# Attention and mixture of experts: group 4's gated rows in the middle stage, final sums partly in halves and partly on TensorE

## What is computed

```python
def _L0_ffn_ref(x, Wg, W1, W2, W3, Ws1, Ws2, Ws3):        # T = 4096 tokens, D = 256, E = 32 experts
    scores = jax.nn.softmax(xf @ Wg, axis=-1)
    weights, indices = jax.lax.top_k(scores, TOP_K)        # TOP_K = 4
    y = jnp.zeros_like(xf)
    for e in range(E):                                     # at most C tokens of each expert
        ...
        out = swiglu(xg, W1[e], W2[e], W3[e]) * w[:, None]
        y = y.at[tok].add(out)
    z = swiglu(xf, Ws1, Ws2, Ws3)                          # the shared expert: silu(x W1) * (x W3) W2
    return (y + z).reshape(B, S, D)

x = x + _L0_xattn_ref(_layernorm(x), ctx, ctx, ...)
x = x + _L0_ffn_ref(_layernorm(x), ...)
```

## Time and profile before

| | |
|---|---|
| median of 3 runs | 789.82 (789.68 to 792.14) |
| the profiled execution | 792.1, its span 790.3 |
| TensorE busy | 747.7 (95%) |
| VectorE busy | 533.0 (67%) |
| ScalarE busy | 465.4 (59%) |
| GpSimd busy | 379.6 (48%) |
| moved by DMA | 164.44 MB, 208 GB/s over the span |
| chain that ended last | TensorE 69%, VectorE 13%, issue 6%, GpSimd 5%, ScalarE 4%, DMA 2% |

### The profile page before, as it was taken

One profiled execution on the slowest core, in us unless ns is written; L12 is line 12 of the kernel. 1 busy time (PEld: TensorE's weight loads), 2 busy tenths in 40 slices (PEclk: granted clock), 3 DMA queues, 4 the chain that ended last, 5 costly groups with the idle time before them and its releaser, 6 DMA issues.

```text
span 790.3 us, 18644 instructions
## 1 busy us (share of the span) xinstructions
PE 747.7 (95%) x4222; PEld 596.3 (75%) x4223; DVE 533.0 (67%) x1683; ACT 465.4 (59%) x1820; POOL 379.6 (48%) x352
## 2 busy tenths in 40 slices
PE   6988999999999999999998959999999999999995
PEld 5766777877777877677775648999999999998555
DVE  4854547575959687686977645666666666665588
ACT  2665777777677868566833204666666666666110
POOL 1002242225747574766567663666666665666000
PEclk9998999999999999999999898999999999999999
DMA  9812072325444454489929788777777675664897
GB/s 311 256 41 63 33 223 96 121 94 170 149 150 140 151 179 136 161 261 355 302 95 367 269 312 265 214 218 246 225 235 240 216 245 182 194 189 142 344 409 323
DMA packets 104734, 164.44 MB, mean 208 GB/s; under 512 B 10902, under 2 KB 87780, under 8 KB 103140
## 3 DMA queue, kind: packets, MB, share of 16 engines
q1 hardware_dynamic: 90447, 120.01, 46.2%
q0 software_dynamic: 13824, 41.96, 14.9%
q10 hardware_dynamic: 404, 1.82, 0.7%
HBM read 90.01 MB, written 78.97 MB: 214 GB/s over the span
## 4 chain that ended last, share of the span: by engine, by line
PE 69%; DVE 13%; issue 6%; POOL 5%; ACT 4%; DMA 2%; DVEq 0%; ACTq 0%; SPq 0%; POOLq 0%
PE psum L1750 19%; PE psum L1639 11%; PE psum L1551 11%; PE psum L1757 9%; PE psum L1487 9%; POOL expert_lists L704 4%; PE psum L1671 4%; PE psum L1510 2%; ACT sm L853 2%; PE psum L1597 2%; DVE big L1450 2%; DVE ln1g L1053 1%; PE psum L1525 1%; DMA expert_lists<-rows,slot 1%; PE psum L1686 1%
## 5 line engine op out<-in xcount | busy, mean ns | idle before, releaser
L744 POOL DMA_INDIRECT y_d<-sm,yrow x160 | 155.1, 970 | 105.7 <-DVE yrow L1426 78.2
L1750 PE MATMUL psum<-xbT,w_now 128*128 128x128 f32 x1280 | 171.2, 277 | 0.2
L704 POOL DMA_INDIRECT expert_lists<-rows,slot x128 | 128.7, 1006 | 72.3 <-issue 36.5
L853 ACT ACTIVATE sm<-psum,nmax 128x77 f32<-128x77 f32 x512 | 158.0, 369 | 6.4 <-DVE nmax L1065 6.3
L1750 PEld LDWEIGHTS psum<-xbT,w_now 128*128 128x128 f32 x1280 | 156.8, 193 | 2.7 <-issue 1.8
L722 POOL TENSOR_TENSOR sm<-sm,sinv 128x1232 f32<-128x1232 f32 x32 | 71.9, 2247 | 173.9 <-DVE sinv L1072 173.8
L1639 PE MATMUL psum<-big,pT 128*128 (+1 forms) x640 | 143.6, 379 | 0.0
L1551 PE MATMUL psum<-big,xnT 128*128 (+2 forms) x384 | 140.6, 516 | 0.0
L1639 PEld LDWEIGHTS psum<-big,pT 128*128 128x128 f32 x640 | 119.1, 190 | 15.0
L853 ACT ACTIVATION_READ_ACCUMULATOR sm<-psum,nmax 128x1 f32 x512 | 128.5, 251 | 0.0
L1551 PEld LDWEIGHTS psum<-big,xnT 128*128 128x128 f32 x384 | 71.3, 192 | 57.4 <-issue 51.7
(11 more groups left out here) (191 smaller groups left out, 972.4 us busy)
## 6 DMA issues: line engine op xcount, KB each, us to landing
xblk<-expert_lists SPq DMA_DIRECT2D x160, 160.0 KB, 2.3
y_d<-zero SPq DMA_DIRECT2D x32, 512.0 KB, 3.8
big<-y_d SPq DMA_DIRECT2D x8, 2048.0 KB, 16.1
big<-in_L_ffn_W SPq DMA_DIRECT2D x16, 320.0 KB, 6.7
xin<-in_x SPq DMA_DIRECT2D x36, 128.0 KB, 2.6
xres<-in_x SPq DMA_DIRECT2D x8, 512.0 KB, 5.8
x_d<-x SPq DMA_DIRECT2D x8, 512.0 KB, 3.3
xn2T_d<-xn2T SPq DMA_DIRECT2D x8, 512.0 KB, 2.9
```

The source lines that it names most:

```text
L704: pool.indirect_dma_start(out=lists, out_offset=bass.IndirectOffsetOnAxis(ap=slot[:, ph, tt, k:k + 1], axis=0), in_=rows[:, ph, tt, :], in ...
L744: pool.indirect_dma_start(out=y_d, out_offset=bass.IndirectOffsetOnAxis(ap=yrow[:, q:q + 1], axis=0), in_=eo[:, q, :], in_offset=None).the ...
L853: last = nc.scalar.activation(sm[:, t % 2, h * SK:(h + 1) * SK], head_scores(h, h + 1), ACT.Exp, bias=nmax[:, t % 2, h:h + 1], accum_out=s ...
L1750: last = mm(bank(2 + q % 2)[:, i * P:(i + 1) * P], w_now[:, q % 2, i, k, :], xbT[:, q % 2, k, :], start=k == 0, stop=k == KC - 1)
```

## The change

There are four parts.

1. *Group 4's gated rows in the middle stage.* `s_up(4, 0)`, `s_up(4, 1)` with their silu and gate now stand in the middle stage, round `s_down(3)`. Their input, the transposed rows of group 4 (512 KB), is loaded by SP right after its fills, on a semaphore of its own, `ld_xg_first`; the load in the expert stage is gone. TensorE and ScalarE wait for both gates of group 4 before the first block. `s_down(4)` opens the final stage, into banks 4 and 5, without a wait for the last expert output.
2. *Halves.* The y rows of groups 0 and 7 are loaded as two DMAs of 1 MB and summed half by half. Group 7 is also stored by halves.
3. *Fourth y row by TensorE.* For groups 5 and 6 VectorE sums three y rows, and the fourth is added to z in PSUM by a product with the identity (`add_rows`).
4. *Orders and banks.* VectorE begins with the sums of group 0 and does the gates of groups 5 to 7 between the sums; `s_down` makes the product with the identity first, 512 columns at a time; z of group 7 goes to banks 0 and 1.

```diff
+        BY_PE, IN_HALVES = (MID + 1, MID + 2), (0, NG - 1)
+        def rows_summed(g):
+            return range(TOPK - 1 if g in BY_PE else TOPK)
...
         def z_bank(g):
-            return 4 if g < MID else 4 + 2 * (g % 2)
+            return 4 if g <= MID else {MID + 1: 6, MID + 2: 4, MID + 3: 0}[g]
@@ SP
             fill_lists(sp, [(0, 8), (8, 16), (16, SP_FILLS)])
+            sp.wait_ge(s["s_psum"], 2 * (MID - 1))
+            sp.wait_ge(s["xn2T_stored"], 16 * (MID + 1))
+            sp.dma_start(xg_end[0], xn2T_d[MID:MID + 1, :, :].rearrange("o p (k n) -> (o p) k n", k=KC)
+                         ).then_inc(ld_xg_first, 16)
             sp.wait_ge(s["tab_ready"], 1)
...
                 load_turn(NG + 2 + g - MID)
+                if g == MID:
+                    continue
...
+                if g in IN_HALVES:
+                    for half in range(2):
+                        tiles = slice(half * TG // 2, (half + 1) * TG // 2)
+                        sp.dma_start(ysum[:, g % RING, tiles, :, :], y_g[:, tiles, :, :]).then_inc(ld_y_half[half], 16)
...
+                if g == NG - 1:
+                    for half in range(2):
+                        sp.wait_ge(s["z_added"], 2 * g + half + 1)
+                        sp.dma_start(out_g[:, tiles, :], final[:, g % RING, tiles, :]).then_inc(stored[g % RING], 16)
@@ ScalarE
             shared_silu(3, 1)
+            shared_silu(MID, 0)
+            shared_silu(MID, 1)
             phase1_over(act)
+            wait(act, "s_gated", 2 * (MID + 1))
@@ VectorE
+            shared_gate(MID, 0)
             add_shared(3)
+            shared_gate(MID, 1)
             phase1_over(dve)
...
+            def add_z(g, half, so_far):
+                p, tiles = g % RING, slice(half * TG // 2, (half + 1) * TG // 2)
+                wait(dve, "ysum_step", sums_done[0])
+                wait(dve, stored[p], g // RING * 16)
+                wait(dve, "z_psum", g * 2 + (half + 1))
+                nc.vector.tensor_tensor(final[:, p, tiles, :], ..., ALU.add).then_inc(s["z_added"], 1)
...
+                if g in IN_HALVES:
+                    for half in range(2):
+                        so_far = sum_rows(g, half, slice(half * TG // 2, (half + 1) * TG // 2))
+                        if g >= MID:
+                            add_z(g, half, so_far)
...
-            shared_gate(MID, 0)
-            shared_gate(MID, 1)
+            sum_group(0)
             shared_gate(MID + 1, 0)
-            sum_group(0)
             sum_group(1)
@@ TensorE
+            def add_rows(g):
+                for half in range(2):
+                    y_loaded(pe, g, half)
+                    mm(bank(z_bank(g) + half).rearrange("p (t d) -> p t d", t=2), ident[:, :],
+                       ysum[:, g % RING, half * TG // 2:(half + 1) * TG // 2, TOPK - 1, :], start=False, stop=True
+                       ).then_inc(s["z_psum"], 1)
...
+            s_up(MID, 0)
             s_down(3)
+            s_up(MID, 1)
...
+            wait(pe, "s_gated", 2 * (MID + 1))
...
-            pe.wait_ge(s["eo_ready"], BLOCKS)
             pe.wait_ge(s["ld_base"], 16 * NG)
-            s_up(MID, 0)
-            s_up(MID, 1)
+            s_down(MID)
             s_up(MID + 1, 0)
-            s_down(MID)
             s_up(MID + 1, 1)
             s_up(MID + 2, 0)
             s_down(MID + 1)
             s_up(MID + 2, 1)
             s_up(MID + 3, 0)
             s_up(MID + 3, 1)
+            add_rows(MID + 1)
             s_down(MID + 2)
+            add_rows(MID + 2)
             s_down(MID + 3)
```

More of the change, by code:

```diff
@@ L281, in attention_moe_kernel @@
         base_stored = [sem(f"base_stored{p}") for p in range(2)]
-        ld_xg_end = sem("ld_xg_end")
+        ld_xg_end, ld_xg_first = sem("ld_xg_end"), sem("ld_xg_first")
+        ld_y_half = [sem(f"ld_y_half{h}") for h in range(2)]
         ld_y = [sem(f"ld_y{p}") for p in range(RING)]
@@ L447, in fill_lists @@
                                   ).then_inc(s["filled"], 16)
-        sums_upto = list(itertools.accumulate(TOPK if g < MID else TOPK - 1 for g in range(NG)))
+        BY_PE, IN_HALVES = (MID + 1, MID + 2), (0, NG - 1)
+        def rows_summed(g):
+            return range(TOPK - 1 if g in BY_PE else TOPK)
+        sums_upto = list(itertools.accumulate(
+            (len(rows_summed(g)) - (0 if g < MID else 1)) * (2 if g in IN_HALVES else 1) for g in range(NG)))
         def summed(eng, g):
@@ L456, in summed, with y_loaded @@
                 eng.wait_ge(s["z_added"], 2 * (g + 1))
+        def y_loaded(eng, g, half):
+            if g in IN_HALVES:
+                eng.wait_ge(ld_y_half[half], 16 * (IN_HALVES.index(g) + 1))
+            else:
+                eng.wait_ge(ld_y[g % RING], 16 * sum(h % RING == g % RING and h not in IN_HALVES for h in range(g + 1)))
         def z_bank(g):
-            return 4 if g < MID else 4 + 2 * (g % 2)
+            return 4 if g <= MID else {MID + 1: 6, MID + 2: 4, MID + 3: 0}[g]
         block = stack.enter_context(nc.Block())
@@ L979, in _ @@
                   packed_table(act, "column", 2, ACT_TURN))
-            for g in range(MID, NG):
+            for g in range(MID + 1, NG):
                 for c in range(KC):
@@ L1665, in s_up @@
                 else:
-                    wait(pe, ld_xg_end, 16 * (NG - MID))
+                    wait(pe, ld_xg_first if g == MID else ld_xg_end, 16 if g == MID else 16 * (NG - MID - 1))
                 wait(pe, "s_gated", (g - 1) * 2 + (c + 1))
@@ L1676, in s_down @@
                 wait(pe, "s_gated", g * 2 + 2)
[L1677 to L1691 removed]
+                hT = sh if g < MID else sh_end[(g - MID) % 2]
@@ new lines, in s_down @@
+                for half in range(2):
+                    z = bank(z_bank(g) + half)
+                    if g <= MID:
+                        wait(pe, "z_added", (g - 1) * 2 + (half + 1))
+                    elif g == MID + 1:
+                        wait(pe, "eo_ready", BLOCKS)
+                    elif g == MID + 2:
+                        wait(pe, "z_added", MID * 2 + (half + 1))
+                    if g >= MID:
+                        tiles = base[:, g * TG + half * TG // 2:g * TG + (half + 1) * TG // 2, :]
+                        mm(z, ident[:, :], tiles.rearrange("p t d -> p (t d)"), start=True, stop=False)
+                    for t in range(half * TG // 2, (half + 1) * TG // 2):
+                        for c in range(KC):
+                            last = mm(z[:, t % 2 * D:(t % 2 + 1) * D],
+                                      hT[:, c, :].rearrange("p (n t) -> p t n", t=TG)[:, t, :], ws2[:, c, :],
+                                      start=c == 0 and g < MID, stop=c == KC - 1 and g not in BY_PE and (g < MID or t % 2 == 1))
+                    if g not in BY_PE:
+                        last.then_inc(s["z_psum"], 1)
+                    elif half:
+                        last.then_inc(s["down_psum"], 1)
```

80 lines of the change are left out of this document (42 added, 38 removed).

## The result

| | kernel before | changed kernel |
|---|---|---|
| median, us | 790.51 (5 runs, 789.68 to 792.14) | 798.26 (4 runs, 796.90 to 800.21) |
| ratio, 95% interval | | 1.0097 [1.0076, 1.0118] |
| profiled execution, us | 792.1 | 800.21 |
| its span, us | 790.3 | 798.5 |
| mean granted TensorE clock | 0.981 | 0.978 |

A fifth run of the changed kernel was disturbed as a whole (its TensorE clock was 0.557) and is left out. The ratio makes the change 7.7 us slower (0.0097 x 790.5; 6.0 to 9.3 by the interval), and the spans of the two profiled executions differ by 8.2. Forecast were +7.8 and a median of 797.6. Nearly everything is lost in the middle joint, and a little comes back at the end.

A forecast was written before the change was run, and what follows sets the result against it. It took TensorE to be busy except at the hole before the expert stage, and transfers to bound the final stage. Middle +9.0, expert stage 0, final -1.2 gave +7.8 on 789.82: 797.6, range 792.0 to 800.5.

The forecast's parts named there:

- middle joint: Between middle and expert stages: first block's transposes 9.8 later, less 0.8 regained at the first blocks, net +9.0.
- rival E: Load lands at 472.5 or later, clock low longer, final stage's waits drop it too: +11 to +12, 801; chance 0.09.
- The queue: Before the expert stage: group 4's load queues behind SP's 21 fills, shares engines evenly with scatters, lands at 471.0.
- The low clock: Middle stage: lower clock after TensorE's standstill adds 2.2 (between 1.1 and 2.8) to group 4's up products and down(3).
- Gate to transposes: From up(4,1)'s end at 484.2, through silu and gate, to the first block's transposes at 485.7: 1.5.
- Given back: Start of expert stage: first blocks run at full clock after 11 microseconds of products, gaining 0.8.
- Final stage: Bound by DMA transfers, so work taken from TensorE and VectorE becomes slack; only its end gains, -1.2.
- Rival C: Final stage bound by the engines, 9.4 gained there; with an early load in the middle, 785.0; chance 0.05.
- D: Middle costs +9.0 and final stage gains -7 to -9.4: 789.4 to 791.8, no change; chance 0.08.
- My tail: End of final stage, after group 3's store lands at 783.0: last sums and half-size store gain 0.9 to 1.5.
- One sign: In the final stage, VectorE idle before groups 1 to 7, with y landings ending the waits; no size given.
- B, the early load: Fills don't hold group 4's load, landing at 466.4: +4.6 in the middle, -1.2 at the end, 793.2; chance 0.13.

## Why the prediction was right

| step | predicted | measured |
|---|---|---|
| load of group 4's rows lands | 471.0 | 472.65 |
| low clock costs the middle work | 2.2 | 1.4 |
| up(4,1) ends | 484.2 | 485.1 |
| first block's transposes | 485.7 | 487.27 |
| given back by the first blocks | 0.8 | 1.65 |
| middle joint, at the third block's up | +9.0 | +9.74 |
| expert stage | 0 | +0.1 |
| final stage | -1.2 | -1.6 |
| sum, of spans | +7.8 | +8.2 |

The path and the waits are the forecast ones, and the loss has the forecast cause. That +9.74 lies so near to +9.0 is in part luck: the load landed outside the prediction's own range (469.8 to 471.8), at a time that it had kept for rival E, and the gate's path was too short, but two clock terms erred the other way.

**The queue.** Right in kind, shown by the load between the fills and by the 4.5 of the kernel without halves. The landing came 1.65 later than summed. The even sharing that the sum assumed was there (45.8% to 44.4% from 468 to 470), and by 471 nearly all of the load was across; the sum had no term for its last 12 packets. It also took the scatters' work to end at 470 and read 470.64 as a landing. That row is the start of the last scatter's transfer, which landed at 473.15: already before, scatters ran to the end of the wait. Why the last packets took until 472.65 is open. The landing also moves between runs of this middle: 472.65 here, 10.5 after the request, and 470.46, 9.3 after it, in the run with one addition.

The prediction weighed what the Trainium skill, "DMA: Bandwidth & Descriptors", section "Queues, rings and completion order", says: that a DMA engine takes a queue's descriptors in ring order. The trace agrees, with 10.5 us from request to landing behind the fills.

**The low clock.** The range was 1.1 to 2.8, and 12.4 us of work (472.68 to 485.1) for 11.0 gives 1.4: half speed ended after 3.1 us of work. Against the same three pieces at full speed in the kernel with the early load, 10.85 (462.28 to 473.13), it is 1.5. The runs with idle products show the cause, and without them up(4,0) shows a higher price, 3.0 for one up product.

**Gate to transposes.** A step that was missing. I had 1.5 from the product to the transposes, from silu and gate alone; it took 2.19. Silu and gate took 1.4 of it, and in the chain stand 0.78 more, in which the engine waited for nothing that the profile shows. All six profiles with this order have 2.20 to 2.23 of idle time there. The likely cause is in the program: TensorE loads a register of the block table before its first transposes, and in the changed order that stands behind the wait for the gate, where before it could be done while the block rows were still under way. That this load is the 0.78 is argued from the code, not tried.

**Given back.** Mis-sized: I had taken 1.55 as a block's time at full speed, but that is with the products of the block before it in between, which the first two blocks don't have. At full speed the two take 2.33, not 3.10. From the first transposes to the third up it was 4.90 before and is 3.25 now, and 3.22 to 3.23 in the five runs with idle products right ahead of the blocks. Landing (+1.65) and the way to the transposes (+0.7) against the two clock terms (-0.8 and -0.85) come to +0.7, the difference between +9.0 and +9.74. That the clock is full at the blocks after 11 us of products held in the changed kernel and in two of its variants (3.25 and 3.26), but not in three others with the same order (4.57 to 4.89), so this gift isn't certain.

**Final stage.** Bound by the transfers, as forecast, and shown by two kernels: 6.9 of TensorE's work put back cost 0.35 at most, half of VectorE's work taken away gave nothing. Rival C (the engines) is excluded, and with it D, of which nothing was seen. Of the 1.6 gained, 1.3 are in the tail (8.7 from the last y rows' landing to the end before, 7.4 now) and 0.4 in the transfers, which is less than they scatter. My tail (0.9 to 1.5) therefore fits. The wait on the store of group 3 stood where I put it (to 792.49), but is worth 0.5 of its 1.66, since the last store is behind three others anyhow. One sign didn't come: VectorE was to stand idle before groups 1 to 7, and it waited for y rows only three times. B, the early load, failed at its condition, for the fills did hold the load; where they were done, it landed 4.5 after its request, within B's 4.0 to 6.2.

**Open.** Why the same kernel takes 791 us in one set and 884 in another, with its engines standing between instructions in the expert stage: the record names the same chip, 8, for both. Then why the load's last packets came so late, what lets the clock fall at the blocks in some runs, and the share of the 0.6 in the tail that is the rearranged order and not chance.

## What to carry to other kernels

Before work is moved into a hole, ask of each transfer that it needs what stands ahead of its request on the queue, and put the request ahead of that backlog: here the same instructions cost some 8 to 10 us or nothing, by one line of SP's order. Then ask what the work was worth where it came from: in a stage in which the DMA share is near 1.0 from the first request to the last landing (0.94 to 1.02 here), engines' work taken away gave nothing, and the filled hole is no gain either. A wait that ends at a store of a full queue can be worth less than its length, here 0.5 of 1.66, because what it releases goes to the end of the same queue.

## What I had not expected of the hardware

- The last packets of a load can come late: from 468 to 470 a load of 512 KB and the scatters beside it had even shares of the engines, by 471 all but 12 of its packets were across, and it landed at 472.65.
- TensorE's half speed came back with either kind of standstill, 7.7 or 10.6 us long, and lasted differently: 6.8 us from 473.15 before, with small products in the second half of it, and 10.2 us from 465.57 now, the last 3.1 of them with large ones. In three runs it came back at the first blocks, behind a wait of only 2.2 with over 10 us of products ahead of it.
- Between the end of the gate and the first block's transposes there were 0.78 us in which nothing was waited for that the profile shows. A register load is the likely cause, not a shown one.
- The kernel before took 790 us in one set and 883 in others, one of them on a chip of the same number. The stage bound by transfers took 47.6 of it in the first set, and in the others 47.4 and 47.9 in its version with idle products: the difference is nearly all elsewhere.
